# Order of VectorE's steps in the last layer's experts, and GpSimd drains in three stages of a two-layer decoder

## The reference, cut to what matters

```python
# x_flat: [2048, 512]; E = 8 experts, TOPK = 2, F_DIM = 352
router_logits = x_flat @ gate_w.T
top_w, sel = jax.lax.top_k(router_logits, TOPK)
top_w = jax.nn.softmax(top_w, axis=-1)
g = jnp.einsum('nd,efd->enf', x_flat, gate_proj)
u = jnp.einsum('nd,efd->enf', x_flat, up_proj)
h = jax.nn.silu(g) * u
eo = jnp.einsum('enf,edf->end', h, down_proj)
out = jnp.einsum('end,ne->nd', eo, tw)     # tw: top_w scattered to [n, E]
```

## Time and profile before

| what | value |
|---|---|
| median of 3 runs | 3454.94 us |
| lowest and highest | 3453.34, 3456.48 us |
| the profiled execution's own time | 3457.22 us |
| its span | 3455.4 us |
| busy, TensorE / VectorE / ScalarE / GpSimd | 3126.9 / 2117.7 / 1291.1 / 1456.0 us |
| mean granted clock of TensorE | 0.954 of full speed |

### The profile page before, as it was taken

The page is one execution under the profiler, slowest core; times in us unless marked ns, Lnnn a source line. Parts: engine busy times, 40 slices in busy tenths (PEclk is TensorE's granted clock), DMA queues, the critical chain, the costliest instruction groups (busy, mean ns, idle before and its releaser), DMA issues. The chain is left out here.

```text
span 3455.4 us, 58053 instructions
## 1 busy us (share of the span) xinstructions
PE 3126.9 (90%) x20720; PEld 2609.3 (76%) x20720; DVE 2117.7 (61%) x3794; ACT 1291.1 (37%) x3291; POOL 1456.0 (42%) x1470
## 2 busy tenths in 40 slices
PE   7999999999969999799896999699999999869991
PEld 5887878878847777677674777488888888758881
DVE  5667566676636667521285777566666678645556
ACT  2343333333346666401212333244444444324430
POOL 4554443344422333310173222355555556444445
PEclk9999999999979999899997999799999999979996
DMA  4001016023410111249573112311101001156664
GB/s 171 18 13 57 0 36 233 0 78 109 151 33 26 45 33 62 93 154 342 164 166 107 40 43 58 126 32 35 35 11 49 11 24 45 43 200 223 224 222 158
DMA packets 137869, 317.13 MB, mean 92 GB/s; under 512 B 18425, under 2 KB 30457, under 8 KB 135538
## 3 DMA queue, kind: packets, MB, share of 16 engines
q1 hardware_dynamic: 120194, 274.61, 23.5%
q0 software_dynamic: 15360, 36.25, 4.0%
q10 hardware_dynamic: 2160, 4.21, 0.3%
HBM read 231.07 MB, written 98.04 MB: 95 GB/s over the span
## 5 line engine op out<-in xcount | busy, mean ns | idle before, releaser
L398 POOL TENSOR_TENSOR a_sq<-a_tq,a_sinq 128x256 f32<-128x256 f32 x128 | 150.4, 1195 | 359.4 <-DVE a_tq L474 358.1
L398 POOL TENSOR_TENSOR a_sk<-a_tk,a_sink 128x256 f32<-128x256 f32 x128 | 123.9, 987 | 90.0 <-DVE a_tk L474 90.0
L364 ACT COPY a_probT<-bank 128x512 f32<-128x512 f32 x64 | 37.5, 586 | 329.0 <-PE bank L713 329.0
L411 POOL TENSOR_TENSOR e_sk<-e_tk 128x512 f32<-128x512 f32 x64 | 66.5, 1039 | 205.5 <-DVE e_tk L501 205.5
L353 ACT ACTIVATE e_prob<-bank,e_nb,e_rq 128x128 f32<-128x128 f32 x256 | 113.8, 455 | 86.6 <-DVE e_nb L575 86.6
L348 ACT ACTIVATE a_sm<-a_sm,a_nmax 128x128 f32<-128x128 f32 x256 | 99.9, 391 | 122.3 <-DVE a_nmax L570 122.3
L952 ACT ACTIVATE b_prob<-bank,b_nb 128x128 f32<-128x128 f32 x512 | 139.1, 386 | 13.6 <-DVE b_nb L1148 13.4
L1046 POOL TENSOR_TENSOR d_prob<-d_prob,d_nmax 128x1024 f32<-128x1024 f32 x32 | 63.9, 1998 | 181.5 <-DVE d_nmax L1143 181.5
L2478 POOL TENSOR_TENSOR n_wu_lo<-nw_wu,n_wu_hi 128x1408 fp32r<-128x1408 f32 x23 | 74.0, 3219 | 136.5 <-DVE n_wu_hi L2522 136.5
L496 DVE TENSOR_TENSOR a_kr<-a_kr,a_sk 128x512 f32<-128x512 f32 x64 | 66.5, 1039 | 89.0 <-POOL a_sk L398 89.0
L1145 DVE TENSOR_REDUCE b_nmax<-bank 128x8 f32<-128x1024 f32 x64 | 77.9, 1218 | 67.6 <-PE bank L1289 63.5
(11 more groups left out here) (542 smaller groups left out, 10762.8 us busy)
## 6 DMA issues: line engine op xcount, KB each, us to landing
packed<-all_zero SPq DMA_DIRECT2D x32, 1024.0 KB, 8.4
cw_wg<-in_c_wg SPq DMA_DIRECT2D x32, 512.0 KB
cw_wu<-in_c_wu SPq DMA_DIRECT2D x32, 512.0 KB
cw_wd<-in_c_wd SPq DMA_DIRECT2D x32, 512.0 KB
nw_wg<-in_f_wg SPq DMA_DIRECT2D x23, 704.0 KB
nw_wu<-in_f_wu SPq DMA_DIRECT2D x23, 704.0 KB
nw_wd<-in_f_wd SPq DMA_DIRECT2D x23, 512.0 KB
nw_xe<-packed SPq DMA_DIRECT2D x46, 256.0 KB, 2.8
```

Of the source, the lines that this page charges most:

```text
L364: nc.scalar.copy(probT[:], pP[:, :]).then_inc(act_pt, 1)
L398: step = nc.gpsimd.tensor_tensor(o, i, s, ALU.mult)
```

## The change

It has two parts.

**Order on VectorE, stage n.** In `slot`, `take_h` of the tile before now stands ahead of `split_gate`. Nothing is added or taken away; in even slots, which have no `split_gate`, the order is as before.

**Three more drains on GpSimd.** `pool.drain()` is called in stage `e` after the last slot's sends (before the normalisations of batches 14 and 15), in stage `b` after the last slot of the last batch (again before those of batches 14 and 15), and in stage `cc` after the normalisation of tile 13. The drains at the ends of the blocks stay.

```diff
@@ wide_attention, gpsimd slot
                 if sends:
                     router.send(pool, (b - 5) // 2, 2 * ((b - 5) % 2) + 1)
+                if router and last:
+                    pool.drain()
@@ narrow_attention, gpsimd slot
                     if e == "n" and older:
                         norm(b - 2)
                         residual(b - 1)
+                if router and s == UN - 1 and not ahead:
+                    pool.drain()
@@ routed_experts, vector slot
                 if ahead:
                     take_x(*following(i, n, R))
+                if back:
+                    take_h(*preceding(i, n, R))
                 if n % 2 and not (isinstance(i, int) and later(i, n) > LAST):
                     split_gate(*((i, 1) if n == 1 else (i + 1, 0)))
-                if back:
-                    take_h(*preceding(i, n, R))
                 dve.wait_ge(act_g, done(t))
@@ combine, gpsimd
                 if b + R < B:
                     gather(b + R)
+                if shared and b == B - 3:
+                    pool.drain()
```

## The result

| | runs | median, us | lowest to highest | profiled run's own time | its span |
|---|---|---|---|---|---|
| before | 4 | 3454.14 | 3452.93 to 3456.48 | 3457.22 | 3455.4 |
| after | 4 | 3431.04 | 3424.46 to 3431.57 | 3431.57 | 3429.8 |

The changed kernel takes 0.993 of the time before (95% interval 0.9916 to 0.9943): 23.1 us less in the medians, 25.7 less in the profiled executions. It is faster; the time lies inside the range and 2.5 us above the forecast of 3428.5.

What follows compares the result with a forecast made beforehand. TensorE, busy 90% of the span, was taken as the bound, with waits for `n_h_lo` in stage n and drains at three stage ends. 19.9 + 6.5 = 26.4 us gives 3430.8, for the median 3428.5 us; range 3424 to 3438.

Steps and rivals of the forecast that it cites:

- Steady odd slots, 16.6 us, less 1.5 for loads: 15.1: Stage n, 21 odd slots: TensorE's wait for `n_h_lo` goes, 16.6 us; later weight loads cost about 1.5 (bounds 0 and 9.5).
- The 13.3 us that the sum took for the other pairs' ways: Stage n: assumed load round trip of the 13 pairs without a wait, beside 13.92 us for one traced.
- The free lateness: Stage n: VectorE may fall 2.3 us behind through late loads before TensorE feels it.
- rival A: Stage n: loads replace the wait, each way 13.92 us, costing 9.5 us; kernel 3436.5 us; chance 0.17.
- First odd slot, 4.8 us: Stage n's first odd slot: 11.49 us falls to 6.68 without its 3.00 us wait, gaining 4.8.
- the upper of the two bounds: First odd slot of stage n: 4.8 us if the slow clock goes too, against 3.3 if it stays.
- Stage n, 19.9 us: Sum for stage n: 16.6 for steady odd slots plus 4.8 for the first, less 1.5 for loads.
- `n_wg_lo` with a median near 1.5 to 1.6 us: VectorE in stage n: sign expected in the changed profile, in place of 3.12 us.
- The drains, 6.5 us: Ends of stages b, e, cc: last drains shrink to 0.66 us, barriers come 3.0 + 1.2 + 2.3 us earlier.
- The new drains, 3.6, 1.8 and 5.2 us: Added GpSimd drains in b, e, cc: lengths at 82 ns a DMA, covered by idle 5.47, 9.57, 8.27 us.
- Rival B: Stage ends: drains give nothing, a block's last drain stays long; gain 19.9 us only, 3435.0 us; chance 0.11.
- Rival C: Stage n: GpSimd's `n_wd_lo` gets in ahead of `n_wg_lo`, +35 us; 24 us slower overall, 3478.6 us; chance 0.04.

Runs made afterwards that it cites:

- experiment 3: Changed kernel with SyncE's second store of a pair moved behind the next pair's loads, so loads issue earlier: 3423.78 us, ratio 0.9923 to before.
- experiment 7: Kernel before (old order, no new drains) with the loads issued early: 3451.66 us, ratio 0.9983 to before.
- experiment 1: Kernel before with the new VectorE order alone, none of the three drains: 3433.36 us, ratio 0.9946 to before.
- experiment 2: Kernel before with the three new drains alone, old order on VectorE: 3445.63 us, ratio 0.9986 to before.
- experiment 10: Changed kernel with the three drains moved behind each stage's last normalisation, uncovered, rerun beside the changed kernel on one chip: 3433.36 us, ratio 0.9943 to before.
- experiment 4: Changed kernel with `split_gate` moved behind `n_h` of the odd slot, so GpSimd's `n_wd_lo` starts first: 3481.06 us, ratio 1.0087 to before.
- experiment 5: The changed kernel run again, on the second chip: 3432.15 us, ratio 0.9924 to before.
- experiment 9: The changed kernel run again, on the third chip: 3428.75 us, ratio 0.9931 to before.
- experiment 6: Changed kernel with the three drains moved behind the last normalisation of b, e and cc, uncovered, second chip: 3434.51 us, ratio 0.9935 to before.

## Why the prediction was right, and where it was off

- *What bounds the kernel.* Right: 18.0 of the 25.6 us are in the stretch where TensorE waited for `n_h_lo`, and the ends of the three stages account for 6.9.
- *Steady odd slots, 16.6 us, less 1.5 for loads: 15.1.* Measured 13.8 (297.2 - 283.43). The wait of the odd slots went as said. The term that was mis-sized is the load's way: it costs 2.8 and not 1.5, shown by experiment 3, where it is taken away: 13.8 + 2.8 are the 16.6. (The 13.3 us that the sum took for the other pairs' ways stood on no row.) The free lateness, put at 2.3 us, is near 2.6: waits of VectorE for up weights of up to 2.61 us cost the next even slot 0.03 at most, the two of 2.77 and 2.78 us 0.2 and 0.3, and the three of 3.18 to 3.34 us some 0.65 each. Between the waits of 1.00 us (at 3107.42) and 3.23 (at 3176.46) lie five pairs, 13.81 us each, where TensorE's pairs take 13.36: the ways were near rival A's 13.92 in that stretch, and over the whole stage a pair took 13.50 (283.43/21).
- *First odd slot, 4.8 us.* Measured 4.8 (11.49 to 6.69). The slow clock behind the wait went with it, the upper of the two bounds. That is partly luck of the execution that before was read from: with the drains alone this slot took 9.34 us and kept the full clock, and in experiment 7 it took 10.46, so the new order's gain here is 2.7 to 4.8.
- *Not in the sum: the first even slot.* It was 8.26 and is 8.85, 0.6 lost. In other executions of the changed kernel it was 8.26 and 9.07, so this is chance and not the change.
- *Stage n, 19.9 us.* Measured 18.0 in the profiled executions, and 17.8 as the order's own gain over before in whole runs; by experiment 1's trace 15.4.
- *`n_wg_lo` with a median near 1.5 to 1.6 us.* Wrong: 2.36. This step of the prediction took `n_wu_lo` where it ended in the earlier trace rows, at 3110.30, but the lateness of the up weights puts it later in most pairs. TensorE's three waits for `n_wg_lo` come from it; the prediction had named such waits as a sign of rival A. With the loads early the median is 1.61, as forecast. The short one is what the change makes possible, and the loads decide whether it comes.
- *The drains, 6.5 us.* Right within what can be measured: 6.9 by the distances to the barriers, 5.6 alone (1.7 to 8), 4.6 and 2.4 for the loss of their cover. The last ones take 0.651 us each, forecast 0.66.
- *The new drains, 3.6, 1.8 and 5.2 us.* In cc it is 5.36 beyond the arithmetic that ended at 1823.54. In b and e they run 4.5 and 2.7 us beyond the last send, 0.9 more than 82 ns a DMA. The cover held: the next statistics of b start at 1425.83, 2.1 us after the drain's end. Timeline of GpSimd in e, after:

```profile
2989.43 0.97 POOL L2080 DMA_INDIRECT packed<-moe_xall,moe_target  x1 [0.30 <-issue]
3000.66 0.19 POOL L431 TENSOR_TENSOR e_rstd<-e_mv,e_eps 128x1 f32<-128x1 f32 x1 [10.26 <-DVE e_mv L558]
```

- *Rival A (loads bind)* is the mechanism of what was lost, at 2.8 of its 9.5 us. *Rival B* is shown wrong by the last drains of 0.651 us in the changed kernel and by experiments 2 and 10. *Rival C* did not happen in the changed kernel, and experiment 4 shows that its mechanism is real: with `n_wg_lo` behind GpSimd each even slot costs 1.94 us, near the 2.2 forecast. Its 35 us over before were too many: the steady slots took 329.5 in place of 297.2, 32.3 more, and 8 of these are the clock's.
- *The whole.* 25.65 us in the profiled executions, forecast 26.4. In medians against the kernel before on the same chip it is 23.1, 25.5 (experiment 5) and 24.2 (experiment 9), so 1 to 3 us less than forecast. The trace gives 1.9 of them to stage n. The rest is within the scatter: stage b alone took 463.2 us in the profile after, 468.6 before, 458.5 with the drains alone and 472.1 with them uncovered (experiment 6; 465.8 in experiment 10), of which the drain of b explains 3.

## What to carry to other kernels

In a list that an engine works off in order, put the short instruction that the bound engine waits for ahead of a long one that has slack, and then work out whether the long one still has its slack where its inputs come latest, not where they come in the slot that you looked at. When a wait goes, the period shortens and whatever goes round with it (here a load that waits for a store that waits for a result) has to be shorter than the new period; here it was a store in an in-order DMA list that could be moved behind the next load. A drain is paid for what was issued since the last one: drain in an idle stretch in front of a stage's end, and it costs nothing there; drain where no idle time is left, and it costs the same as before. And read more than one execution before a term is taken from it: here the first odd slot and the stages ahead of n differed between executions by as much as some terms of the sum.

## What the runs showed of the hardware

- A GpSimd drain behind indirect DMAs takes 82 ns for each DMA since the drain before, and some 0.65 us more where arithmetic has just been issued: 2467 ns for 22, 4268 for 44, 5897 for 64. With none since, it takes 651 ns behind arithmetic and 41 right behind another drain. Dispatched right behind a send, it took some 0.9 us more (b, e). The Trainium skill (VectorE: DVE Perf Modes, section The DRAIN you can't avoid) speaks of a constant of about 12 ns on all five engines for drains at a kernel's start and end. In the trace after the other engines' drains at the kernel's start took 7 to 10 ns, near that, and GpSimd's 169 ns. The drains at the ends of stages are neither of the two, and GpSimd's took 651 to 5897 ns there, or 41 behind another drain.
- VectorE's and GpSimd's instructions with two operands in SBUF shut each other out both ways: VectorE's 1.6 us become 3.54 when GpSimd began 0.33 us earlier, and whenever it overlapped GpSimd's `n_wu_lo` in the changed kernel it ended 1.48 us behind it. GpSimd's lets VectorE in between two instructions that stand back to back (3.62 us become 5.01). The Trainium skill (SBUF — State Buffer, section SBUF: two separate sides) calls the shared port pair an exclusive lock for the whole instruction, which agrees.
- In the kernel with the late gate the granted clock fell from 1.00 to 0.50 (1.2 GHz) for about 3 us in five even slots in a row, each time right behind a wait of 1.7 us, and cost 1.6 us each. In the even slots ahead of them and after them it stayed at 1.00 behind waits as long. In the old order it fell behind waits of 3.00 us (before) and 2.67 us (experiment 7) and not behind one of 2.40 us (experiment 2). No run tells why.
